# Deformable convolution on one core: the stage of row weights removed, the weights made by GpSimd inside the main loop

## The reference, cut to what matters

```
om     = conv3x3(x, w_off) + b_off            # 27 channels per pixel
off_y, off_x, mask = om[:, :9], om[:, 9:18], sigmoid(om[:, 18:])
py = off_y + row + ky - 1;  px = off_x + column + kx - 1      # for each of 9 taps
sampled = bilinear(x, py, px) * mask          # 16 channels x 9 taps per pixel, zero outside
out = einsum('bckhw,ock->bohw', sampled, w) + b
return relu(batchnorm(out)) + x
```

## Time and profile before

| | us |
|---|---|
| median of 3 runs | 2331.4 (2331.2 to 2337.84) |
| span of the profiled execution | 2334.2 |
| busy: PE / DVE / ACT / POOL | 1539.5 / 1558.4 / 1449.8 / 606.7 |
| from the block of row weights to the main loop's block | 351.5 to 671.5 |

### The profile page before, as it was taken

One profiled execution on the slowest core, in us unless ns is written; L12 is line 12 of the kernel. 1 busy time (PEld: TensorE's weight loads), 2 busy tenths in 40 slices (PEclk: granted clock), 3 DMA queues, 4 the chain that ended last, 5 costly groups with the idle time before them and its releaser, 6 DMA issues. The chain is left out here.

```text
span 2334.2 us, 61913 instructions
## 1 busy us (share of the span) xinstructions
PE 1539.5 (66%) x24206; PEld 1050.0 (45%) x24207; DVE 1558.4 (67%) x1718; ACT 1449.8 (62%) x2219; POOL 606.7 (26%) x1168
## 2 busy tenths in 40 slices
PE   4755980000008888888898898898888898891620
PEld 4632330000006666666665566666665666660310
DVE  5342006656717888888888788888887888883105
ACT  2221224344218898888898898898887898890102
POOL 2000000000033444444443444444444444430000
PEclk9688995555558999999999999999999999996555
DMA  2177874667675666666666666566666656640008
GB/s 116 32 190 184 233 218 159 215 227 275 235 214 126 151 147 157 149 149 155 150 148 152 148 149 157 149 150 157 149 146 150 152 147 157 149 100 22 3 0 338
DMA packets 288861, 362.19 MB, mean 155 GB/s; under 512 B 61853, under 2 KB 260820, under 8 KB 285014
## 3 DMA queue, kind: packets, MB, share of 16 engines
q1 hardware_dynamic: 209552, 226.57, 37.6%
q0 software_dynamic: 36864, 59.94, 11.2%
q10 hardware_dynamic: 42182, 72.05, 9.0%
HBM read 253.94 MB, written 104.39 MB: 154 GB/s over the span
## 5 line engine op out<-in xcount | busy, mean ns | idle before, releaser
L758 POOL DMA_DIRECT2D rows<-scratch_parts x1152 | 583.1, 514 | 821.1 <-PE ps_even_y L790 798.8
L799 PE MATMUL ps_odd_y<-rows,sel 32*128 32x504 f32 (+2 forms) x928 | 459.8, 496 | 502.5 <-DMA rows<-scratch_parts 345.2
L939 DVE TENSOR_TENSOR G<-odd_y,ps_odd_v 128x1008 f32<-128x1008 f32 (+2 forms) x464 | 542.0, 1168 | 182.5 <-PE ps_odd_v L816 182.4
L816 PE MATMUL ps_odd_v<-tent_x,stage 32*128 32x171 f32 (+2 forms) x5568 | 591.1, 318 | 0.0
L947 DVE TENSOR_TENSOR G<-even_v,ps_even_y 128x1008 f32<-128x1008 f32 (+2 forms) x464 | 539.3, 1162 | 23.6 <-ACT even_v L895 21.7
L816 PE MATMUL ps_even_v<-tent_x,stage 32*128 32x171 f32 (+3 forms) x5568 | 541.9, 324 | 8.5 <-DMA stage<-scratch_xt 8.3
L889 ACT COPY odd_y<-ps_odd_y 128x504 f32<-128x504 f32 (+2 forms) x928 | 526.4, 567 | 21.4 <-PE ps_odd_y L799 17.1
L895 ACT COPY even_v<-ps_even_v 128x1008 f32<-128x1008 f32 (+2 forms) x464 | 450.2, 970 | 134.6 <-PE ps_odd_v L816 126.5
L834 PE MATMUL ps_r<-G,conv_w 128*32 128x224 f32 (+1 forms) x8832 | 483.3, 346 | 13.2 <-ACT res L900 13.1
L799 PEld LDWEIGHTS ps_odd_y<-rows,sel 32*128 32x128 f32 x928 | 173.0, 186 | 689.8 <-issue 350.5
L816 PEld LDWEIGHTS ps_odd_v<-tent_x,stage 32*128 32x128 f32 x5568 | 477.8, 190 | 0.0
(11 more groups left out here) (134 smaller groups left out, 913.5 us busy)
## 6 DMA issues: line engine op xcount, KB each, us to landing
place<-scratch_px SPq DMA_DIRECT2D x960, 105.0 KB, 3.4
scratch_parts<-parts ACTq DMA_DIRECT2D x18, 3136.0 KB, 16.7
rows<-scratch_parts POOLq DMA_DIRECT2D x960, 52.5 KB, 3.4
x<-scratch_xh SPq DMA_DIRECT2D x48, 406.0 KB, 5.9
place<-scratch_px SPq DMA_DIRECT2D x192, 84.0 KB, 2.7
scratch_om<-om ACTq DMA_DIRECT2D x64, 196.0 KB, 7.1
rows<-scratch_parts POOLq DMA_DIRECT2D x192, 42.0 KB, 2.6
scratch_conv<-res SPq DMA_DIRECT2D x448, 14.0 KB, 1.8
```

The costliest lines, as they stand in the source:

```text
L758: pool.dma_start(bass.AP(tensor=rows[b][:].tensor, offset=32 * g * pitch + here, ap=[[2 * pitch, Y_KINDS], [GROUP * W, 3], [1, count * W]] ...
L799: nc.tensor.matmul(ps_odd_y[:, lo:hi], sel[32 * g:32 * g + 32, :], taps(rows, 32 * g, 32, p, lo, hi), start=True, stop=True).then_inc(odd_ ...
L816: m = nc.tensor.matmul(sub(ps_v[g // 2], 0, 128, i * 512 + lo + first, dims), stage[32 * g:32 * g + 32, j * IMAGE + v * C:j * IMAGE + (v + ...
L939: nc.vector.tensor_tensor(two(G, ROW, v, slot(v)), two(odd_y[p % 3], ROW, v), two(ps_v[1], 512, v), ALU.mult).then_inc(odd_weighted, 1)
```

## The change

The stage of row weights goes. The convolution and the main loop become one block, whose tiles share memory: the convolution's input and output lie in the ring `G` of the loop, which shrinks from 20 to 18 rows and now runs on across pairs.

- **Convolution part.** The 27 channels are reordered so that each kind (column px, row offset oy, mask) is stored by view: even and odd views apart. Per chunk ACT now takes a sigmoid of all channels and DVE evacuates the same chunk with a bias and pattern added. Per pair DVE makes two ranges and merges both results. The output goes out in 24 small DMAs per pair instead of 4: half by SP, half by ACT, and ACT issues those of pair n after its sigmoids of pair n+1. ACT may start pair n+2 only when those of pair n have landed (the same two buffers).
- **Row weights.** POOL makes them for pair it+2 while the loop works on pair it, from a dense read-back of oy and mask: nine clips of 464 elements, then a subtraction, an addition and a product of 3712 elements each. Only 8 planes are stored, and each is read twice (as high and as low). POOL then splits them on chip, per 10 steps ("double"): three products with the 0/1 vector `is_low` and three subtractions, each of 840 elements.
- **Queues in the loop.** SP issues `rows` (48 per pair now), `place` (24 per pair now, 72 before), the dense loads (2) and the store of the weights (1) beside what it had. POOL issues no DMA.
- **Before and after.** The transform stores 18 small blocks of zeros into `om`. The windows stage reads ranges in another form (2 loads of short runs) and takes 18 loads instead of 3 for `xrows`; its sigmoid goes.

The diff, cut to its core (the last loop is ACT's in the convolution part; lines 492 to 607 go as a whole):

```diff
-                    nc.scalar.activation(sorted_rows(mask[b]), by_parity(logit[b]), ACT.Sigmoid).then_inc(masked, 1)
-                    for r in range(WIN):
-                        a = nc.scalar.activation(sorted_rows(tent_y[b], r), by_parity(oy[b]), ACT.Abs, bias=shift[:, r:r + 1])
-                    a.then_inc(distant, 1)
...
-                    nc.scalar.copy(kinds(parts[b], 0, WIN), kinds(tent_y[b], 0, WIN)).then_inc(high, 1)
...
-                    nc.vector.tensor_scalar(tent_y[b][:, :], tent_y[b][:, :], 1.0, 1.0,
-                                            ALU.min, ALU.subtract).then_inc(capped, 1)
...
+            def tents(pair):
+                    pool.wait_ge(dense_loaded, 32 * (pair + 1))
+                    wait(pool, parts_stored, 16 * pair)
+                    for k in range(WIN + 1):
+                        at = float(k - BASE_SHIFT - 1)
+                        nc.gpsimd.tensor_scalar(tent_y[:, k * DCH:(k + 1) * DCH], dense_y[:, :], at, at + 1.0,
+                                                ALU.max, ALU.min).then_inc(clipped, 1)
+                    pool.wait_ge(clipped, (WIN + 1) * (pair + 1))
+                    w = tent_y[:, 0:WIN * DCH]
+                    nc.gpsimd.tensor_tensor(w, w, tent_y[:, DCH:], ALU.subtract).then_inc(differed, 1)
+                    pool.wait_ge(differed, pair + 1)
+                    nc.gpsimd.tensor_scalar(w, w, 1.0, None, ALU.add).then_inc(raised, 1)
+                    pool.wait_ge(raised, pair + 1)
+                    w = sub(tent_y, 0, 128, 0, [[DCH, WIN], [1, DCH]])
+                    nc.gpsimd.tensor_tensor(w, w, sub(dense_m, 0, 128, 0, [[0, WIN], [1, DCH]]), ALU.mult).then_inc(weighted, 1)
...
+                    def take_high(k):
+                        n = 3 * double + k
+                        wait(pool, rows_ready, n - 1)
+                        nc.gpsimd.tensor_scalar(high[n % 2][:, :], r[k].bitcast(fp32), is_low[:, 0:1], None, ALU.mult
+                                                ).then_inc(high_ready, 1)
+                    def take_rest(k):
+                        n = 3 * double + k
+                        pool.wait_ge(high_ready, n + 1)
+                        nc.gpsimd.tensor_tensor(r[k], r[k].bitcast(fp32), high[n % 2][:, :].bitcast(fp32), ALU.subtract
+                                                ).then_inc(rows_ready, 1)
...
+                tents(0)
+                tents(1)
+                split(0)
+                for double in range(1, ALL_DOUBLES):
+                    split(double)
+                    if double % DOUBLES == 1 and double // DOUBLES + 2 < PAIRS:
+                        tents(double // DOUBLES + 2)
...
+                for pair in range(PAIRS):
+                    b = pair % 2
+                    wait(act, om_stored[b], 16 * STORES * (pair // 2))
+                    for ch in range(NCH):
+                        act.wait_ge(convolved, pair * NCH + ch + 1)
+                        nc.scalar.activation(sub(G, 0, 128, SIG_AT[b] + ch * CH, [[1, CH]]), ps_o[ch % 2][:, 0:CH],
+                                             ACT.Sigmoid, bias=boff[:, 0:1]).then_inc(masked, 1)
+                    if pair:
+                        act.wait_ge(merged, pair)
+                        store_om(act, pair - 1, 1)
...
-G_SLOTS = 20
+G_SLOTS = 18
```

More of the change, by code:

```diff
@@ new lines, in load_rows @@
+                def load_rows(double):
+                    pair, b = double // DOUBLES, double % ROW_BUFFERS
+                    for half in range(2):
+                        first, count = BATCHES[2 * (double % DOUBLES) + half]
+                        for low in range(2):
+                            for g in range(4):
+                                parity, i = g // 2, g % 2
+                                sp.dma_start(sub(rows[b], 32 * g + 16 * half + 8 * low, WIN, 0,
+                                                 [[GROUP * W, KK], [1, count * W]]).bitcast(fp32),
+                                             dram("parts", (pair * 2 + i) * KIND + parity * KK * SL + first * W,
+                                                  [[B * KIND, WIN], [SL, KK], [1, count * W]])).then_inc(rows_loaded[b], 16)
@@ L763, in _ @@
[L763 to L772 removed]
+                pool.wait_ge(consts_loaded, 16 * len(LOADS))
@@ new lines, in split @@
+                def split(double):
+                    b = double % ROW_BUFFERS
+                    third = 3 * GROUP * W
+                    r = [rows[b][:, k * third:(k + 1) * third] for k in range(3)]
+                    pool.wait_ge(rows_loaded[b], 16 * 16 * (double // ROW_BUFFERS + 1))
+                    def take_high(k):
[8 more added lines that the diff above has]
+                                                ).then_inc(rows_ready, 1)
+                    take_high(0)
+                    take_high(1)
+                    take_rest(0)
+                    take_high(2)
+                    take_rest(1)
+                    take_rest(2)
@@ L789, in spread_even @@
                     for i in range(2):
-                        m = nc.tensor.matmul(ps_even_y[:, i * 512 + lo:i * 512 + hi], sel[32 * i:32 * i + 32, :],
-                                             taps(rows, 32 * i, 32, p, lo, hi), start=True, stop=True)
+                        which, what = row_weights(it, p, i, lo, hi)
+                        m = nc.tensor.matmul(ps_even_y[:, i * 512 + lo:i * 512 + hi], which, what, start=True, stop=True)
                     m.then_inc(even_spread, 1)
@@ L797, in spread_odd @@
                     lo, hi = columns(2 * p + 1)
-                    g = 2 + i
-                    nc.tensor.matmul(ps_odd_y[:, lo:hi], sel[32 * g:32 * g + 32, :], taps(rows, 32 * g, 32, p, lo, hi),
-                                     start=True, stop=True).then_inc(odd_spread, 1)
+                    which, what = row_weights(it, p, 2 + i, lo, hi)
+                    nc.tensor.matmul(ps_odd_y[:, lo:hi], which, what, start=True, stop=True).then_inc(odd_spread, 1)
                 def sample(it, p):
@@ L931, in room @@
                     elif p in (0, half):
-                        wait(dve, reduced, BLOCKS * (it - 1) + (p + G_SLOTS) // half + 1)
+                        wait(dve, reduced, BLOCKS * (it - 1) + (p + STEPS - G_SLOTS // 2) // half + 1)
+                    if it == 0 and p == half:
+                        for b in range(2):
+                            dve.wait_ge(om_stored[b], 16 * STORES * PAIRS // 2)
                 def weight_odd(it, p):
```

541 lines of the change are left out of this document (259 added, 282 removed).

## The result

The changed kernel takes **2963.69 us** (2962.07 to 2978.81, 6 runs), the kernel before on the same chip 2334.62: ratio 1.271, 95% interval [1.267, 1.275]. The forecast said slower by 53 us (2384, range 2110 to 2450); it is slower by 629.

The account below looks back on a forecast made before the run. No engine was full; DVE's 2.94 us step cycle, with 0.29 us slack, bounds the loop. 2334.2 - 255 + 15 + 8 = 2102, less 2.8 gives 2099; plus 285 for POOL against caps gives 2384 us, range 2110 to 2450.

Parts of the forecast that it names:

- Where the change decides: Main loop: whether DVE's caps wait for a whole POOL instruction; the upper mechanism was taken, with break-even at 232 us.
- Rival 1: Main loop: POOL's arithmetic leaves caps at 417 ns and steps at 2.94 us; time 2099 us, chance 0.22.
- Its price, +285: Main loop: caps waiting behind POOL cost 210 us beside tents and 75 beside splits (bounds +200 to +444).
- POOL keeps up: Main loop: POOL's tents 24 and splits 24 us fit a pair of 87; split due at 59 us ends near 45.
- rival 3: Main loop: POOL becomes late and PE waits for rows at steps 0, 10 and 20; 2480 to 2550 us, chance 0.07.
- The DMA term, +8 (0 to 35): Main loop: added dense loads and weight stores pass ahead of result stores, adding a quarter to ACT's 35 us wait.
- The 35 us that I took for res before: Main loop before the change: ACT's wait for result stores, taken as 12.4 x 2.8 over the loop.
- Ahead of the loop, -255: Transform and convolution: first weighting moves from 701.9 to 447 us, at 14 us per pair; bounds 200 to 280 gain.
- The transform's share: Transform: 18 more DMAs at its start add 9 us, moving the first convolution matmul from 206.4 to 215.4.
- Behind the loop, +15: Windows stage: range loads in short runs and 15 more row loads, less savings, cost 15 us (0 to 25).

Follow-up runs that it names:

- cap_one_port: Changed kernel with the cap's input laid out in three runs of 168 elements, so DVE can't take two at a time: 2768.3 us, ratio 1.189.
- pool_tiny: Changed kernel with every POOL instruction of tents and splits cut to 8 columns, DMAs and waits kept: 2736.0 us, ratio 1.175.
- two_results_paired_caps: Changed kernel with 16-partition rows loads, three convolution buffers, later tents, dense loads and parts store, two result buffers; caps still paired: 2602.8 us, ratio 1.117.
- rows_16_one_port_conv3: Changed kernel with 16-partition rows loads, cap input in three runs, and three convolution output buffers: 2617.7 us, ratio 1.120.
- one_port_dense_res_act: Changed kernel with cap input in three runs, and dense loads and result stores issued by ACT, not SP: 2921.8 us, ratio 1.253.

## Why the prediction came out wrong

1. **Where the change decides.** "A cap which comes while POOL reads or writes waits until POOL's instruction ends": right, shown by the two timelines, by cap_one_port and by pool_tiny. The Trainium skill ("SBUF — State Buffer", Who interferes with whom) says this, and here the trace agrees: caps of up to 8256 ns beside POOL's instructions of 8.1 and 9.65 us, and the products L956 and L964, which don't move two elements at a time, untouched at 1.19 us. Rival 1 is out.
2. **Its price, +285.** Caps are longer by 352 us; removing the effect gives 191 to 237 us. The 191 and 237 come from one-port caps, which each take 0.26 us longer than free paired ones, so they are lower bounds; pool_tiny gives 223. The two-input instructions took 8.08 as taken (8.1). The one-input ones were mis-sized: I took 1.0 ns per element from a memset, and L681 takes 9.65 us where I had 3.7, L675 1754 ns (0.46), L695 2432 (0.84). So POOL is busy 82 us a pair in place of 48, and clips no longer hide in the slack. That the net is near 285 all the same is luck: with the measured lengths my own steps would give some 550. What brought it back is that the splits hardly hurt (some 70 us of longer caps, where these steps give 200 with the measured lengths) and that caps overlap other waits.
3. **POOL keeps up.** It failed as soon as the caps and loads were mended: tents of 42 us stood ahead of a split due at step 20, which came 8 to 17 us late in 14 of the pairs, 13 on the mean (rival 3's mechanism). In the changed kernel slower steps hid it.
4. **The DMA term, +8 (0 to 35).** This is the step that failed. Place waits 231 us and res 162, and mending the two by width, order and a second buffer is worth (1.271 - 1.117) x 2334 = 360 us (two_results_paired_caps), of which the third convolution buffer is 14 to 23 (as it gained alone and in rows_16_one_port_conv3). I counted issues ("the count is equal") and bytes, and not how wide a load is: `rows` fills 8 partitions where the kernel before filled 16, half of the DMA engines, 23 us for each double's rows in the one queue that also carries place and res; and the dense loads seem to use two engines. I also dropped POOL's queue as free, when it had kept rows apart from place; no run moved them back. The 35 us that I took for res before is 27.6 in the trace.
5. **Ahead of the loop, -255.** It is -127, the second term that failed. The period is 22 us, not 14, 8 x 14 = 112 of the missing 128. The issues took 0.75 us each, not 0.5 (+3); the chunk chain 7.7, not 5.7 (+2), PE's mean clock from 198 to 560 us being 0.74; the landing 3.0 to 8.9, not 1.8 (+3 in the middle). The transform's share was right: the first convolution matmul starts at 217.5, where I had 215.4.
6. **Behind the loop, +15.** It is +10. (Its parts as I listed them add up to 17.)

## What to carry to other kernels

Where a small instruction moves two elements at a time on VectorE, as the cap does here, a long GpSimd instruction beside it made it wait to that instruction's end; before giving GpSimd work, count the elements of its longest instruction against the step's slack, or lay the small one's input out in pieces. When loads move to another queue or change their shape, price the width (here 8 partitions in place of 16 halved the rate) and what stands behind it on the same queue and engines, not the number of issues. Where one engine's work is two doubles ahead, write down when its input lands and when its output is due before placing a long piece between.

## What the runs showed that I had not expected

- GpSimd's one-input instructions are slower per element than its two-input ones: 9.65 us against 8.08 for 3712 elements, 2432 ns against 1980 for 840, and 1754 ns for 464 with two operations. A memset was 0.87 ns per element.
- Loads over 8 partitions moved some 54 GB/s with half of the DMA engines busy, those over 16 partitions twice as much.
- Issuing a DMA can hold the engine that issues it: four small stores took ACT 17.18 us, where the median of one is 0.44.
- Added DMA traffic can make TensorE wait for its own program: gaps with no releaser, 0 before, 78 and 93 us in the two kernels nearest to it, nearly all ending 1.2 to 2.0 us behind an instruction packet.
- Single costs did not add up: -191 and -199 gave -330 together, and taking two waits away in one_port_dense_res_act made it 150 us slower than cap_one_port.
